# The last image of a routed-expert kernel goes to its experts in two halves, and the first expert weights are read ahead of the second rows

## The reference

```python
t = t + attn(ln(t))                      # 8 heads, causal, 1024 tokens an image
flat = ln(t).reshape(-1, 128)
probs = softmax(flat @ router_w.T)       # 8 experts
topk_probs, topk_idx = top_k(probs, 2)
gates = topk_probs / (sum(topk_probs) + 1e-9)
y_e = (silu(flat @ w1[e].T) * (flat @ w3[e].T)) @ w2[e].T
t = t + sum_over_two(gate * y_e)
```

## Time and profile before

| | |
|---|---|
| Median of 3 runs | 2342.59 us (2337.69 to 2347.49) |
| The profiled execution, its own time | 2342.18 us |
| Its span, first to last instruction | 2340.0 us |
| Last product of attention, start | 1941.39 us |
| Last scatter of rows, start | 1989.22 us |
| First product of the experts, start | 2002.54 us |
| PE busy over the span | 2130.8 us |

### The profile page before, as it was taken

How to read it: one execution, slowest core, us unless ns; L and a number is a source line. 1 busy time by engine, 2 the same in 40 slices (tenths; PEclk the granted TensorE clock), 3 DMA queues, 4 the chain that set the end, 5 groups by cost and what they waited for, 6 DMA issues and landing times. The chain is left out here.

```text
span 2340.0 us, 39728 instructions
## 1 busy us (share of the span) xinstructions
PE 2130.8 (91%) x11827; PEld 1730.1 (74%) x11827; DVE 1659.3 (71%) x4246; ACT 1297.1 (55%) x2669; POOL 1529.1 (65%) x1444
## 2 busy tenths in 40 slices
PE   4789999999977999999999999999999992899994
PEld 2466666666656888888888888888888882688883
DVE  4889888787647677777877778778787773344444
ACT  3667666666423666666666666666666661233331
POOL 2679778777732666586785876867859675355551
PEclk9999898887878999999999999999999995899996
DMA  1950000000000001010010100100101001555555
GB/s 47 387 207 10 10 10 1 10 1 1 19 19 10 1 2 26 1 42 4 7 38 1 39 7 5 41 1 11 35 1 43 3 8 43 178 194 190 195 172 215
DMA packets 135400, 130.92 MB, mean 56 GB/s; under 512 B 82885, under 2 KB 101359, under 8 KB 135190
## 3 DMA queue, kind: packets, MB, share of 16 engines
q1 hardware_dynamic: 124950, 107.12, 15.0%
q0 software_dynamic: 9088, 17.07, 2.1%
q10 hardware_dynamic: 1152, 4.19, 0.4%
HBM read 64.78 MB, written 65.10 MB: 56 GB/s over the span
## 5 line engine op out<-in xcount | busy, mean ns | idle before, releaser
L1278 POOL TENSOR_TENSOR plo<-pf,phi 128x512 fp32r<-128x512 f32 (+1 forms) x640 | 751.9, 1186 | 338.2 <-ACT phi L1506 304.6
L1504 ACT ACTIVATE pf<-psum 128x512 f32<-128x512 f32 (+1 forms) x640 | 357.3, 558 | 411.3 <-PE psum L1339 303.9
L1506 ACT ACTIVATE phi<-psum 128x512 fp32r<-128x512 f32 (+1 forms) x640 | 355.0, 555 | 0.0
L1650 DVE CUSTOM_DVE_ANT_0 psum<-psum,ahead_wide 128x128 f32<-128x128 f32 (+3 forms) x512 | 247.1, 503 | 69.1 <-PE psum L1392 64.7
L1337 PE MATMUL psum<-phi,x_tok 128*128 128x512 f32 (+1 forms) x640 | 265.9, 416 | 5.5 <-POOL plo L1278 5.5
L1931 POOL DMA_INDIRECT chosen<-yg,xg x156 | 152.8, 979 | 154.4 <-DVE yg L2043 115.3
L1392 PE MATMUL psum<-xT,qT 128*128 128x512 f32 (+3 forms) x768 | 244.9, 347 | 4.3 <-DVE peak L1650 3.3
L1337 PE MATMUL psum<-qT,xT 128*128 128x512 f32 (+1 forms) x640 | 237.6, 371 | 2.2 <-ACT phi L1506 1.3
L1338 PE MATMUL psum<-plo,x_tok 128*128 128x512 f32 (+1 forms) x640 | 237.7, 371 | 0.0
L1339 PE MATMUL psum<-phi,x_tok 128*128 128x512 f32 (+1 forms) x640 | 237.4, 371 | 0.0
L1338 PE MATMUL psum<-qT,xT 128*128 128x512 f32 (+1 forms) x640 | 236.2, 369 | 0.0
(11 more groups left out here) (304 smaller groups left out, 5262.0 us busy)
## 6 DMA issues: line engine op xcount, KB each, us to landing
wg<-turned_w SPq DMA_DIRECT2D x39, 874.0 KB
routed<-empty SPq DMA_DIRECT2D x1, 34056.0 KB, 96.0
xg<-routed SPq DMA_DIRECT2D x39, 264.0 KB
qT<-nmax SPq DMA_DIRECT2D x512, 0.5 KB, 2.0
y<-chosen SPq DMA_DIRECT2D x8, 1024.0 KB, 10.3
turned_w<-wT SPq DMA_DIRECT2D x8, 874.0 KB, 4.4
x_in_sb<-in_x SPq DMA_DIRECT2D x8, 512.0 KB, 3.3
out<-o_st ACTq DMA_DIRECT2D x8, 512.0 KB, 5.6
```

Of the source, the lines that this page charges most:

```text
L1278: g_.tensor_tensor(plo[:, T % RP, 0:n], pf[:, T % RF, 0:n], phi[:, T % RP, 0:n].bitcast(F32), ALU.subtract).then_inc(a["low_ready"], 1)
L1504: s_.activation(pf[:, T % RF, 0:n], bank[T % RS][:, 0:n], ACT.Exp)
L1506: s_.activation(phi[:, T % RP, 0:n], bank[T % RS][:, 0:n], ACT.Exp).then_inc(a["high_ready"], 1)
L1650: last = v.tensor_tensor_reduce(out=source[:, col:col + n], in0=source[:, col:col + n], in1=ahead_wide[:, HALF - n:HALF], scale=1.0, scala ...
```

## The change

The last image, number 7, becomes two units, U1 with its tiles 0 to 3 and U2 with its tiles 4 to 7. Every routing function takes a unit and works on its tiles alone. The other seven images are units of eight tiles and keep their steps.

U1 needs only quarters 0 and 1 of the last pair, so `statistics` waits for four additions fewer. Its statistics stand at step 15 of the last pair on DVE, its deviations at step 16 on POOL, its normalising at step 18 on DVE. What remains of U1 and all of U2 stands in one more pair of steps (g = 32) in place of four, in a new function `last_routing` on DVE and in new lines on the others. The semaphore for scatters is split: `scattered_late` counts the second half of image 6, so that U1's tiles of `rows` wait only for the first half. In the table at the start of the experts, `weights_of(0)` is issued ahead of `rows_of(1)`.

```diff
+            ROUTED = [(b, 0, NC) for b in range(B - 1)] + [(B - 1, 0, NH1), (B - 1, NH1, NC)]
+            NU = len(ROUTED)
+            U1, U2 = NU - 2, NU - 1
...
-                return (b if 0 <= b < B else None), g % PAIRS
+                return (b if 0 <= b < B - 1 else None), g % PAIRS
...
-            T0, T1 = -NP, (NG_ + PAIRS + 1) * NP
+            T0, T1 = -NP, (NG_ + 1) * NP
+            LASTG = NG_ - 1
...
+                if (g, p) == (NG_, 0):
+                    yield "rows", B - 1, 0
+                if (g, p) == (NG_, 2):
+                    yield "route", U1
+                if (g, p) == (NG_, 7):
+                    yield "rank", U1
+                if (g, p) == (NG_, 9):
+                    yield "rows", B - 1, 1
+                if (g, p) == (NG_, 10):
+                    yield "route", U2
+                if (g, p) == (NG_, 12):
+                    yield "rank", U2
...
+                    def deviations(u):
+                        b, c0, c1 = ROUTED[u]
+                        pool.wait_ge(r["mvb_ready"], u + 1)
                         if b:
                             pool.wait_ge(r["x2_ready"], b * NC)
-                        g_.tensor_tensor(rsb[:, :], mvb[:, :, 1], epst2[:, 0:1].to_broadcast([P, NC]), ALU.add).then_inc(r["veb_ready"], 1)
-                        pool.wait_ge(r["veb_ready"], b + 1)
-                        g_.tensor_tensor(rsb[:, :], rsb[:, :], mhalf2[:, 0:1].to_broadcast([P, NC]), ALU.pow).then_inc(r["rsb_ready"], 1)
-
-                    def scatter(b, n):
-                        c, k = n // KINDS, n % KINDS
+                        g_.tensor_tensor(rsb[:, c0:c1], mvb[:, c0:c1, 1], epst2[:, 0:1].to_broadcast([P, c1 - c0]), ALU.add
+                                         ).then_inc(r["veb_ready"], 1)
+                        pool.wait_ge(r["veb_ready"], u + 1)
+                        g_.tensor_tensor(rsb[:, c0:c1], rsb[:, c0:c1], mhalf2[:, 0:1].to_broadcast([P, c1 - c0]), ALU.pow
+                                         ).then_inc(r["rsb_ready"], 1)
...
+                                              ).then_inc(r["scattered_late"] if b == B - 2 and c >= NH1 else r["scattered"], 16)
...
+                        if (g, p) == (LASTG, 16):
+                            deviations(U1)
+                        if (g, p) == (NG_, 14):
+                            deviations(U2)
+                        if (g, p) == (NG_, 15):
+                            for n in range(KINDS * NH1):
+                                scatter(U1, n)
+                        if (g, p) == (NG_, 16):
+                            for n in range(KINDS * NH1):
+                                scatter(U2, n)
+                    pool.wait_ge(r["scattered"], 16 * KINDS * (NC * B - NH1))
+                    pool.wait_ge(r["scattered_late"], 16 * KINDS * NH1)
...
+                    def rank(u):
+                        b, c0, c1 = ROUTED[u]
+                        to = side_bank(r["rank_drained"], u + 1)
+                        pe.wait_ge(r["both_ready"], u + 1)
...
+                        t.matmul(to[:, c0 * E:c1 * E], below_bf[:, :], both[:, c0 * E:c1 * E], start=True, stop=False)
+                        for d in range(1, c1 - c0):
+                            t.matmul(to[:, (c0 + d) * E:c1 * E], ones_bf[:, :], both[:, c0 * E:(c1 - d) * E], start=False, stop=False)
+                        t.matmul(to[:, c0 * E:c1 * E].rearrange("p (c e) -> p c e", e=E), ones_bf[:, :],
+                                 before[:, u % 2, :].unsqueeze(1).to_broadcast([P, c1 - c0, E]), start=False, stop=True
...
+                        if (g, p) == (NG_, 0):
+                            copy_rows(B - 1, 0)
+                        if (g, p) == (NG_, 1):
+                            second_copy(U1)
+                        if (g, p) == (NG_, 2):
+                            exponents(U1)
+                        if (g, p) == (NG_, 9):
+                            copy_rows(B - 1, 1)
+                            second_copy(U2)
+                        if (g, p) == (NG_, 10):
+                            exponents(U2)
...
+                        dve.wait_ge(a["out_added"], 2 * NQ * PAIRS * (b + 1) - (NQ if b == B - 1 and half == 0 else 0))
...
+                            if u == U1:
+                                dve.wait_ge(r["scattered"], 16 * KINDS * (NC * b - NH1))
+                            elif u == U2:
+                                dve.wait_ge(r["scattered_late"], 16 * KINDS * NH1)
...
+                    def choose(u):
+                        shares(u)
+                        top(u, first, best, 0)
+                        top(u, first, best, 1)
+                        without_first(u)
+                        top(u, second, best2, 0)
+                        top(u, second, best2, 1)
+                        chosen_two(u)
+
+                    def place_rows(u):
+                        gates(u)
+                        ranks(u)
+                        slots(u)
+                        counts(u)
+
+                    def last_routing(g, p):
+                        if (g, p) == (LASTG, 15):
+                            statistics(B - 1, 0)
+                            aggregates(U1)
+                        if (g, p) == (LASTG, 18):
+                            normalise(U1, range(0, NH1))
+                        if (g, p) == (NG_, 1):
+                            peaks_off(U1)
+                        if (g, p) == (NG_, 2):
+                            choose(U1)
+                        if (g, p) == (NG_, 7):
+                            statistics(B - 1, 1)
+                            aggregates(U2)
+                        if (g, p) == (NG_, 8):
+                            place_rows(U1)
+                        if (g, p) == (NG_, 9):
+                            normalise(U2, range(NH1, NC))
+                        if (g, p) == (NG_, 10):
+                            peaks_off(U2)
+                        if (g, p) == (NG_, 11):
+                            choose(U2)
+                        if (g, p) == (NG_, 12):
+                            place_rows(U2)
...
                     rows_of(0)
+                    weights_of(0)
                     rows_of(1)
-                    weights_of(0)
                     for g in range(NG):
```

More of the change, by code:

```diff
@@ L1447, in rank @@
                         pe.wait_ge(r["below_made"], 1)
-                        if b:
-                            pe.wait_ge(r["before_ready"], b)
-                        t.matmul(to[:, 0:NC * E], below_bf[:, :], both[:, :], start=True, stop=False)
-                        for d in range(1, NC):
-                            t.matmul(to[:, d * E:NC * E], ones_bf[:, :], both[:, 0:(NC - d) * E], start=False, stop=False)
-                        t.matmul(to[:, 0:NC * E].rearrange("p (c e) -> p c e", e=E), ones_bf[:, :],
-                                 before[:, b % 2, :].unsqueeze(1).to_broadcast([P, NC, E]), start=False, stop=True
+                        if u:
+                            pe.wait_ge(r["before_ready"], u)
@@ new lines, in chosen_two, with gates @@
+                    def chosen_two(u):
+                        b, c0, c1 = ROUTED[u]
+                        if u:
+                            dve.wait_ge(r["rank_ready"], u)
+                        v.tensor_tensor(both[:, c0 * E:c1 * E].rearrange("p (c e) -> p c e", e=E), first[:, c0:c1, :], second[:, c0:c1, :],
+                                        ALU.add).then_inc(r["both_ready"], 1)
+                    def gates(u):
+                        b, c0, c1 = ROUTED[u]
+                        step(v.tensor_tensor(den[:, c0:c1], best[:, c0:c1], best2[:, c0:c1], ALU.add))
+                        step(v.tensor_scalar(den[:, c0:c1], den[:, c0:c1], 1e-9, None, ALU.add))
+                        step(v.reciprocal(den[:, c0:c1], den[:, c0:c1]))
+                        v.tensor_tensor(rows[:, 0, c0:c1, P], best[:, c0:c1], den[:, c0:c1], ALU.mult)
+                        v.tensor_tensor(rows[:, 1, c0:c1, P], best2[:, c0:c1], den[:, c0:c1], ALU.mult).then_inc(r["rows_ready"], 1)
```

189 lines of the change are left out of this document (97 added, 92 removed).

## The result

The changed kernel took 2321.20 us (median of 15 runs, 2314.03 to 2335.49) against 2339.68 us (15 runs, 2333.14 to 2347.49) for the kernel before in the same rounds. The ratio is 0.9931, with a 95% interval of 0.9914 to 0.9949: faster by 16 us, 12 to 20. The profiled execution took 2318.47 us, its span is 2316.8 us.

A forecast was written before the change was run, and what follows sets the result against it. It took the 60.5 us gap between attention and experts as the bound: some 10.1 us from fewer end scatters plus 1.9 from earlier U2, weights 0, gave 12.1; 2342.2 - 12.1 = 2330 us, range 2324 to 2338.

The forecast's parts named there:

- eight scatters less behind the last slots: POOL between attention and experts: only U2's eight scatters remain at the end, some 10.1 us of the 12.1 gained.
- the pause behind the table of groups is still there [...]: 2.9 more: POOL, U2's scatters: the pause that ended with DVE's table was expected to recur there, adding 2.9 us, to 1978.1.
- it is now DVE's chain, not the pile of scatters, that starts them: U2's scatters: POOL is free by 1965.4, so U2's slots, ready at 1964.6, start them 0.8 us later.
- DVE's chain: DVE after attention: choice, gates and slots for U1, then U2; U2 ready at 1964.6 and not 1966.5, worth 1.9 us.
- the other end that I named: POOL's deviations in the last pair: four columns take half of 1.67 us, making the shift 1.2 instead of 2.0.
- Attention's end: PE, last pair: attention's last piece ends at 1945.5, 3.5 us later, behind U1's route and POOL's shifted low parts.
- The weights: Expert start: first weights read ahead of second rows; at best 1.1 us earlier, at worst 1.1 later, taken as 0.
- the lower case: Expert start: second rows land only with the weights, leaving PE's turning still to do, 1.1 us later.
- Shut out during U2's choice: Rival, chance 0.20: DVE's choice for U2 holds up U1's scatters on POOL; gain 7 us, time 2335.
- Shut out in every dense stretch: Rival, chance 0.04: any dense DVE stretch holds up POOL's scatters, image 6's included; 1.3 us slower, 2343.5.
- Image 6's scatters land late: Rival, chance 0.10: U1's normalising waits for their landing, up to 4.1 us, holding the chain 2.1 longer; gain 10, 2332.
- No pause at all: Rival, chance 0.12: no pause in U2's scatters on POOL, which end at 1975.2; gain 15 us, time 2327.

The follow-up runs named there:

- run 5: The kernel before, with the last image's 16 scatters made to wait for DVE's table of groups; untimed, last scatter ended at 1259.0 us from the first scores.
- run 10: The kernel before, with five more scatters to an unread tensor in image 0's pair; untimed, pause of 3.14 us behind the tenth of the last sixteen.
- run 11: The kernel before, with one more scatter to an unread tensor behind image 0's; untimed, last scatter at 1253.6 us from the first scores.
- run 12: The changed kernel with five more scatters to an unread tensor behind image 0's; untimed, last scatter ended at 1243.7 us from the first scores.
- run 2: The changed kernel with the second rows read ahead of the first weights, so the halves alone; 2316.79 us, ratio 0.9934 to the kernel before.
- run 3: The kernel before with the first weights read ahead of the second rows, nothing else; 2335.52 us, ratio 1.0004.
- run 4: The changed kernel with PE's turning of the second group behind the first up-products, not ahead of them; 2322.19 us, ratio 0.9952 to the kernel before.
- run 1: The changed kernel again, with no edit; 2322.73 us, ratio 0.9953 to the kernel before.
- run 9: The kernel before, with image 7's deviations on POOL ahead of image 6's last scatter; untimed, pause of 3.15 us behind the first of the sixteen.

## Why the prediction was wrong

The sign and the place were right, and so was the main term, eight scatters less behind the last slots. The sum fell short by 3.9 us at the last scatter (12.1 forecast, 16.0 in the profile), and one step makes most of that.

**The step that failed** is "the pause behind the table of groups is still there [...]: 2.9 more". I took one pause, ended 0.1 us after DVE's table, as made by DVE. It belongs to POOL's train of scatters: it comes with DVE idle (run 5), stands behind U1's first scatter in the changed kernel, and of all that was tried only scatters added ahead moved it (runs 10 to 12). In the changed kernel it is 1.87 us instead of 3.14 and falls in U1's batch. There it delays eight scatters that were going to be early: U2's slots were ready at 1955.34, U2's first scatter started at 1956.30, and the least such delay is the 0.28 of run 12. So the pause cost 0.7. With it fails "it is now DVE's chain, not the pile of scatters, that starts them": U2's first scatter came straight behind U1's last. From U2's slots to the last scatter's end I had 1964.6 to 1978.1, 13.5 us; it took 10.8. That is 2.7 of the 3.9.

**DVE's chain** was 0.7 shorter than forecast: U2's slots stood 18.4 behind the end of attention, where I had 19.1. U1's first scatter started 0.3 behind its slots, where I had taken the 0.8 behind the last gate in the earlier trace rows, and the power on four columns took 1.04 and not the full 1.67 (the other end that I named). Against it went U1's normalising: 2.44 us, where I had taken half of 2.15. U2's took 1.11. U1's starts 0.09 behind a pair of POOL's low parts that last to 1930.72. Its first two tiles took 0.71 and 1.30 and each ended 0.09 behind one of the two low parts; the last two took 0.34 each. So it is in all eight profiles with halves (2.36 to 2.49 in sum). The Trainium skill, SBUF — State Buffer, on who interferes with whom, says that DVE, in a mode that uses two ports, and GpSimd share a port pair as an exclusive lock, so that one waits out the other's instruction. The 0.09 behind each low part agree with it; no run took POOL's parts away to prove it.

**Attention's end**, +3.5 forecast, was +3.0: the full shift on POOL (2.0) was 1.3. That is the last 0.5 of the 3.9.

**The weights** were worth nothing, as forecast (runs 2 and 3: between 0.5 worse and 0.2 worse by the final sum, inside the spread). The second rows did land late, as the lower case said (4.11 us of waiting at 1978.47), and the 2.0 us by which PE started earlier in run 4 didn't reach the end.

**The rivals.** *Shut out during U2's choice* is excluded: seven scatters were issued from 1947.42 to 1956.0 at pauses of 0.30 or 0.31, and DVE's choice for U2, with its operations on two SBUF inputs, ran from 1950.3 to 1953.6 among them at 0.19 to 0.21 each. The rule that the prediction took from the Trainium skill, SBUF — State Buffer, on who interferes with whom, that an operation with two SBUF inputs contends with a GpSimd instruction that reads SBUF, had no effect to be seen on either. The same section of the Trainium skill adds, as an inference, that making a transfer's descriptors on GpSimd needs the write side while such an operation takes only the read side; by that the two need not meet here, and the rows agree. *Shut out in every dense stretch* falls with it: image 6's scatters ran at pauses of 0.30 through U1's choice (1935.5 to 1939.5). *Image 6's scatters land late*: U1's normalising waited last for POOL's power in the profile above and for the landing in runs 1 and 4, with 1.9 to 2.5 us of idle time either way, so the two come at nearly the same time. In runs 1, 4 and 9 the landing came 1.4 to 1.5 us behind the scatter's end, 2.4 to 2.5 behind its start, so the bound of 4.1 was not reached. The fixed cost of about 2.0 us that the prediction cites from the Trainium skill is somewhat short of that. *No pause at all*, gain 15 and 2327 us, was nearest, for another reason than it gave: there is a pause, but in a place where it costs only 0.7.

**The range.** Its lower end was the no-pause case less 3 us. The profile's own gain of 15.8 would give 2342.2 - 15.8 = 2326.4 from the execution I anchored at, inside the range. The median of 2321.2 lies lower because the kernel before itself has a median of 2339.7 in the longer timing, 2.5 below the anchor, and because this timing's ratio is at the favourable side of what the two timings show (16 and 11 us). That last part is luck of the timing. So of the 8.9 us between 2330.1 and 2321.2 the sum made 3.7, the anchor 2.5, and this timing's spread the other 2.7. The start of the first scores lay between 719.4 and 742.3 us over all profiles, and nothing in the change acts on it; I had allowed 2 us for that.

**What stays open** is what makes the pause. It comes after a number of scatters that moves by three for one more and by fourteen for five more, so it is not a plain count of them. Nothing in the traces shows POOL waiting for a semaphore in it. I didn't find why it is 3.14 us in one kernel and 1.7 to 1.9 in another. The expert stage has one of its own: its 156 indirect transfers to `chosen` pause for 2.16 us behind the 113th, in all fourteen profiles, also in those with scatters added in attention. In the kernel before:

```profile
2221.26 0.98 POOL L1931 DMA_INDIRECT chosen<-yg,xg  x1 [2.46 <-DVE yg L2043]
2224.40 0.98 POOL L1931 DMA_INDIRECT chosen<-yg,xg  x1 [2.16 <-issue]
```

In kernels without added scatters both pauses thus stand behind the 113th transfer of their stage. That speaks for something that comes round in POOL's indirect transfers and starts anew between the stages; it is a guess, and the 116 and 127 of runs 10 to 12 don't follow from it.

## What to carry to other kernels

When the last piece of routed work has no cover, cut it in two and let the first half's long serial tail (here 16 transfers at 1.27 us) run beside the second half's decision chain: the end is then the second half's slots plus its own transfers, if the first half's are out by then (here they were 0.7 us late). Before a stall is tied to the engine that happened to finish beside it, ask what else fits it; one coincidence in one trace is no cause, and here it decided which half was charged 2.9 us. For a kernel whose first stage spreads by 20 us, count marks from the start of the stage that changed, and give the range of the whole time that spread as well.

## What the hardware showed that I had not expected

- A train of indirect transfers of 128 rows from POOL runs at 1.26 to 1.27 us each, with one idle time of 3.13 to 3.15 us in it (1.66 to 1.87 with halves, 0.88 in run 12), with DVE idle as well as busy. Scatters added some 950 us earlier move it. The expert stage's train has one of 2.16 us behind its 113th transfer.
- DVE's normalising of four tiles took 2.36 to 2.49 us beside POOL's low parts and 1.11 beside POOL's scatters: the scatters cost DVE nothing that shows, and POOL's low parts double the time.
- POOL's power took 1.04 us for 4 columns and 1.67 for 8, by my estimate from these two 0.16 us a column above a base of 0.4.
- The stage before attention took 719 to 742 us in fourteen profiles of kernels that are alike up to there; PE's mean granted clock in it was 0.89 in the shortest and 0.85 in the longest.
